# Cross attention in split fp32: the matmul operands' addresses modulo 512 bytes are changed by the order of declaration

## The reference

```
x_q = (w_qk y)^T;  x_k = w_qk x;  x_v = w_v x + b_v
energy = x_q x_k                        # 1024 x 1024
attention = softmax(energy, rows)
attention = attention / (1e-07 + sum of attention over its rows, per column)
x_r = x_v attention
out = x + relu(w_t (x - x_r) + b_t)
```

## Time and profile before

| | |
|---|---|
| median of three runs | 1870.97 us (1868.31 to 1871.37) |
| profiled execution, its own time | 1869.64 us |
| its span, first to last instruction | 1867.7 us |
| TensorE matmuls in it | 8884, busy 1859.1 us (100%) |
| VectorE, ScalarE, GpSimd busy | 81%, 70%, 42% of the span |
| mean granted TensorE clock | 0.999 |

### The profile page before, as it was taken

The page is one execution under the profiler, slowest core; times in us unless marked ns, Lnnn a source line. Parts: engine busy times, 40 slices in busy tenths (PEclk is TensorE's granted clock), DMA queues, the critical chain, the costliest instruction groups (busy, mean ns, idle before and its releaser), DMA issues.

```text
span 1867.7 us, 26374 instructions
## 1 busy us (share of the span) xinstructions
PE 1859.1 (100%) x8884; PEld 1562.4 (84%) x8884; DVE 1506.9 (81%) x2036; ACT 1300.3 (70%) x1793; POOL 780.5 (42%) x415
## 2 busy tenths in 40 slices
PE   9999999999999999999999999999999999999999
PEld 7888888888888888888888888888888888888887
DVE  6888787887877878878778788787787877877878
ACT  6677766677666776667766677766677666776664
POOL 4542444533444334444244452444533444424430
PEclk9999999999999999999999999999999999999999
DMA  3111111011120111111111111111011111111100
GB/s 107 46 46 46 68 67 64 26 45 68 67 68 25 61 49 67 68 45 45 45 67 68 53 37 45 67 68 67 23 54 59 68 67 35 55 45 68 68 12 34
DMA packets 33947, 101.92 MB, mean 55 GB/s; under 512 B 4209, under 2 KB 4977, under 8 KB 33905
## 3 DMA queue, kind: packets, MB, share of 16 engines
q1 hardware_dynamic: 33360, 101.46, 15.7%
q10 hardware_dynamic: 544, 0.00, 0.0%
HBM read 67.90 MB, written 33.55 MB: 54 GB/s over the span
## 4 chain that ended last, share of the span: by engine, by line
PE 96%; DVE 2%; ACT 1%; issue 0%; DMA 0%; SPq 0%; DVEq 0%
PE pv L693 36%; PE row_b L601 19%; PE row_a L601 14%; PE pv L669 9%; PE row_a L661 5%; PE row_b L661 5%; PE row_a L652 4%; PE row_b L652 4%; DVE colsum L445 0%; DMA x_sb<-x 0%; DVE p_sb L427 0%; DVE p_lo L452 0%; PE pv L661 0%; DVE gx_lo L387 0%; DVE s_part L464 0%
## 5 line engine op out<-in xcount | busy, mean ns | idle before, releaser
L201 POOL TENSOR_TENSOR y_lo<-y_raw,y_hi 128x896 fp32r<-128x896 f32 x128 | 279.1, 2202 | 567.5 <-ACT y_hi L258 378.4
L452 DVE SCALAR_TENSOR_TENSOR p_lo<-p_sb,row_inv,p_hi 128x1024 fp32r<-128x1024 f32 x256 | 329.4, 1288 | 96.7 <-ACT p_hi L304 96.7
L287 ACT ACTIVATE ev<-row_b 128x512 f32<-128x512 f32 x384 | 228.5, 595 | 195.1 <-PE row_b L601 195.1
L186 POOL TENSOR_TENSOR x_lo<-x_sb,x_hi 128x1024 fp32r<-128x1024 f32 x63 | 152.5, 2422 | 447.1 <-ACT x_hi L246 447.1
L296 ACT ACTIVATE p_sb<-p_sb,neg_max 128x1024 f32<-128x1024 f32 x256 | 295.1, 1154 | 46.8 <-DVE neg_max L427 42.7
L304 ACT ACTIVATE p_hi<-p_sb,row_inv 128x1024 fp32r<-128x1024 f32 x256 | 292.4, 1142 | 32.8 <-PE pv L693 30.7
L445 DVE SCALAR_TENSOR_TENSOR colsum<-p_sb,row_inv,colsum 128x1024 f32<-128x1024 f32 x224 | 289.6, 1293 | 8.5 <-DVE row_inv L435 0.6
L693 PE MATMUL pv<-p_lo,z_hi 128*128 128x512 f32 x1024 | 273.9, 389 | 0.5 <-DVE p_lo L452 0.5
L693 PE MATMUL pv<-p_hi,z_hi 128*128 128x512 f32 x1024 | 273.9, 389 | 0.0
L693 PE MATMUL pv<-p_hi,z_lo 128*128 128x512 f32 x1024 | 273.7, 389 | 0.0
L693 PEld LDWEIGHTS pv<-p_lo,z_hi 128*128 128x128 f32 x1024 | 192.0, 188 | 41.1 <-DVE p_lo L452 1.3
(11 more groups left out here) (128 smaller groups left out, 3592.5 us busy)
## 6 DMA issues: line engine op xcount, KB each, us to landing
x_sb<-x SPq DMA_DIRECT2D x64, 512.0 KB, 4.1
out<-res SPq DMA_DIRECT2D x62, 512.0 KB, 2.9
y_raw<-y SPq DMA_DIRECT2D x64, 256.0 KB, 3.6
y_raw<-y SPq DMA_DIRECT2D x32, 512.0 KB, 3.7
out<-res SPq DMA_DIRECT2D x4, 256.0 KB, 2.0
res<-w_qk SPq DMA_DIRECT2D x1, 256.0 KB, 3.6
res<-w_t_T SPq DMA_DIRECT2D x1, 256.0 KB, 7.3
res<-w_v SPq DMA_DIRECT2D x1, 256.0 KB, 7.4
```

What stands on the lines that cost most here:

```text
L186: nc.gpsimd.tensor_tensor(x_lo[par][:, kt, :], x_sb[par][:, kt, :], x_hi[par][:, kt, :].bitcast(FP32), ALU.subtract).then_inc(x_lo_done, 1)
L201: nc.gpsimd.tensor_tensor(y_lo[:, :, cols], y_raw[:, 1:8, cols], y_hi[:, :, cols].bitcast(FP32), ALU.subtract).then_inc(y_lo_done, 1)
L287: nc.scalar.activation(ev[:, to, :], bank_b, ACT.Copy, scale=scale).then_inc(b_copied, 1)
L452: nc.vector.scalar_tensor_tensor(out=p_lo[r][:, :], in0=p_sb[r][:, :], scalar=row_inv[:, j:j + 1], in1=p_hi[r][:, :].bitcast(FP32), op0=AL ...
```

## The change

It moves the declarations of the operands' tiles, and adds two that nothing uses, one of 64 bytes and one of 384 bytes per partition. No instruction is changed but for its addresses. The tiles x_sb to res keep their order among themselves and come first; behind them stand the 64 bytes, g, wtT, y and z, then the 384 bytes, hnT, and the small tiles.

```diff
-        g_hi, g_lo = sb("g_hi", [P, KT, C], FP32R), sb("g_lo", [P, KT, C], FP32R)
-        hnT_hi, hnT_lo = sb("hnT_hi", [P, KT, C], FP32R), sb("hnT_lo", [P, KT, C], FP32R)
-        wtT_hi, wtT_lo = sb("wtT_hi", [P, KT, C], FP32R), sb("wtT_lo", [P, KT, C], FP32R)
...
-        y_hi, y_lo = sb("y_hi", [P, 7, BANK], FP32R), sb("y_lo", [P, 7, BANK], FP32R)
...
-        z_hi, z_lo = sb("z_hi", [P, NT, C], FP32R), sb("z_lo", [P, NT, C], FP32R)
...
         res = sb("res", [P, KT, N])
 
+
+        sb("gap_stationary", [P, 16])
+        g_hi, g_lo = sb("g_hi", [P, KT, C], FP32R), sb("g_lo", [P, KT, C], FP32R)
+        wtT_hi, wtT_lo = sb("wtT_hi", [P, KT, C], FP32R), sb("wtT_lo", [P, KT, C], FP32R)
+        y_hi, y_lo = sb("y_hi", [P, 7, BANK], FP32R), sb("y_lo", [P, 7, BANK], FP32R)
+        z_hi, z_lo = sb("z_hi", [P, NT, C], FP32R), sb("z_lo", [P, NT, C], FP32R)
+        sb("gap_hnT", [P, 96])
+        hnT_hi, hnT_lo = sb("hnT_hi", [P, KT, C], FP32R), sb("hnT_lo", [P, KT, C], FP32R)
         bv_sb, bt_sb = sb("bv_sb", [P, KT]), sb("bt_sb", [P, KT])
```

## The result

The changed kernel takes 1903.37 us (median of 5 runs, 1903.01 to 1904.30) against 1870.73: ratio 1.0178, 95% interval 1.0168 to 1.0189. It is slower by some 33 us; the forecast was 1800, in a range of 1774 to 1875. The span went from 1867.7 to 1901.0 us at the same granted clock.

The account below looks back on a forecast made before the run. The prediction took TensorE's matmul spacing to bound the kernel: 1869.6 us less 96 for shorter spacing plus 25 for new waits gave 1798.6, or 1800 as a median of runs, range 1774 to 1875.

Parts of the forecast that it names:

- What bounds the kernel: TensorE's matmuls cover the whole span, so time is their number times their spacing, 226.7 ns for 512 columns, 120.0 for 256.
- The two streams fall on the same part of the memory and the moving one loses 32 cycles in each load: On TensorE, moving reads and the next weight load were said to collide, costing 13.3 ns per matmul, 118 us in all.
- gross gain of 96 us: Shorter TensorE spacing before waits: 79.5 us from 512-column matmuls and 16.6 us from 256-column ones.
- one cycle per 16 bytes: Argument for the collision on TensorE: the extra 32 cycles equal one cycle for each 16 bytes of the weight load.
- small end: If TensorE matmuls without a weight load show the collision's whole share, the gain is 13.4 us, giving 1858.
- The best end of 215.7 ns: Spacing of fp32 matmuls on zeros, 2.4 ns above 512 cycles, taken as what TensorE's 512-column matmuls would reach (215.8).
- the slow clock: At 1.2 GHz TensorE's spacing was 426.7 ns, 512 columns with nothing on top; taken as support for the collision.
- What is late next: Two places that fit TensorE closely were to become waits as it got faster, giving back 25 us.
- (a): End of a batch: the next batch's p1 waits for VectorE's z_lo, 0.55 us 31 times, 17 us.
- (b): p6 of the second pair waits longer for ScalarE's copy of row_b, 0.26 us 31 times, 8 us.
- The slower rival: 64 bytes bring TensorE's streams one collision more, 233 ns spacing for good, +59 us less 4 of waits: 1926; chance 0.19.
- No change: Rival: TensorE's 13.3 ns are not a collision of these two reads, so time stays 1869 to 1872; chance 0.26.

Follow-up runs that it names:

- e13: Kernel before with g, wtT, y and z set 256 bytes from their moving operands modulo 512, hnT as x: 1870.17 us, ratio 1.0000.
- e10: Kernel before plus series of 24 matmuls behind its end, stationary slice starting s 4-byte elements behind moving (level: s = 0): 226.7 ns level, 232.9 at 64 bytes.
- e14: Kernel before plus matmul series behind its end with 128, 96, 64 and 32 stationary columns; level, 512 moving columns: 226.7 ns with 128, 231.3 with 32.
- e7: Kernel before with only hnT moved, to 64 bytes below x modulo 512: 1866.36 us, ratio 0.9979.
- e15: Kernel before plus matmul series behind its end, moving widths 512 down to 128, level and 64 bytes off; 220.0 ns for widths 500 to 484 when off.

## Why the prediction was wrong

- *What bounds the kernel*, and that the change moves nothing but addresses: right. So was that steps of 512 bytes leave 226.7 as it is; a distance of 256 bytes does too (e13, s = 64).
- *"The two streams fall on the same part of the memory and the moving one loses 32 cycles in each load"*: this step failed. In place of the gross gain of 96 us the long matmuls lost 45.5 us and the short ones gained 8.6. For 512 columns level slices are the best place, not the worst: 226.7 ns, which no place in e10 beats by more than 0.1, against 233.3 at 64 bytes. The extra does not follow the load's size (e14). That it equalled one cycle per 16 bytes was a coincidence of one size. The earlier trace rows pointed that way: without a load under it a matmul lasted 1 or 4 ns less. I noted it as an argument against and priced it as the small end only.
- *The best end of 215.7 ns*, from fp32 matmuls at half the rate: not reached in any series of 512 fp32r columns (226.6 is the least). A spacing of another data rate was no bound for this one. Nor was the slow clock: that the extra is absent there is true, but it does not say that the extra can be had at full speed.
- *What is late next*, (a) and (b): not met, since TensorE became slower. z_lo's idle time ahead of it grew, 0.25 us to 0.46, and (b) went the other way, -2.9 us:

```profile
959.55 1.23 DVE L415 TENSOR_TENSOR z_lo<-row_b,z_hi 128x1024 fp32r<-128x1024 f32 x1 [0.46 <-ACT z_hi L285]
```

- *The slower rival* came nearest: the 233 ns that the earlier trace rows showed wherever the phase is moved became the mean spacing. Its reason, one collision more, is not shown. Its 1926 was 23 too high by its own terms: 7,296 x 6.67 = 48.7 us for the long matmuls measured 45.5, since some were already off 226.7 before; the 10.2 us for the short ones measured -8.6; and the waits gave 2.9 back. The short matmul at 0.11 us in the earlier trace rows could have been read as a sign that 256 and 512 columns go opposite ways.
- *No change*: by the Trainium skill (SBUF — State Buffer, "Who interferes with whom") the two read ports of TensorE, for the moving operand and for weight loads, are independent; I took from it that addresses do not count. The measurement decides: with nothing but addresses changed the spacing of 512 columns moves by 6.3 ns and the time by 1.8%. That a port or a bank is what couples them is not shown.

Open: why level places give 512 columns the lowest steady spacing but not 256 columns, and why a series settles at one of several spacings. e10 shows that neither distance alone sets the spacing, not how they act together. The cause of the 33 us is shown down to the spacings; what makes the spacings is not.

## What to carry to other kernels

When TensorE is the bound and the spacing of matmuls is above their columns, measure the spacing for the wanted place and width in a series by itself before laying out tiles: here level starts suited 512 fp32r columns, and 64 bytes off suited 256 columns, for 4 us of 1870 (e7). Then check in the kernel itself: the same distance gave 113.6 or 117.8 ns there. An extra that fits a formula at one size is a guess; vary the size. And where the trace has a matmul without the suspected partner, let its row weigh more than the fit.

## What the runs showed of the hardware

- fp32r matmuls with a weight load each, at a granted clock of 0.999: 226.7 ns for 512 columns and 120.0 for 256 with level starts; with others 226.6 to 234.4 for 512 and 113.3 to 122.5 for 256 (e10, e15).
- A distance of 256 bytes is as level (s = 64: 226.7; e13 within 0.1% of before), and one of 4 bytes is not (s = 1: 232.4). That all places repeat every 256 bytes is not shown: with 256 columns s = 16 had 117.8 in both passes and s = 80, 256 bytes further, 113.4 and 113.3.
- One steady spacing for several widths (220.0 ns for 484 to 500 columns, 64 bytes off), and a dependence on how a series is entered (s = 48: 233.3 and 228.7 for one and the same series; z halves of the changed kernel: 113.6 or 117.8).
